# Two passes of a batch loop written out, with the second batch's first norm and queries placed among the first batch's last MLP steps, and a setup loaded in order of use

## The reference

```python
def reference(x, ctx, cond, ...):
    # L0: adaptive norm (scale, bias from silu(cond) @ Wss_q), cross attention to the
    #     context (16 heads of 16; keys, values from an adaptive norm of ctx), residual
    x = _L0(x, ctx, cond)
    # L1: norm, scores of each token against 64 prototypes (q @ k, softmax, @ v),
    #     combined = [norm, evidence, anchor]; router softmax over 3 experts,
    #     h = silu(combined @ e_w1 + b), h @ e_w2, sigmoid gate, output projection, residual
    x = _L1(x, cond, ctx)
    # L2: modulated norm, self attention over 1024 tokens, cross attention, gelu MLP of 1024
    x = _L2(x, cond, ctx)
    # L3: modulated norm, windowed self attention (rolled by 64), cross attention to the
    #     16 best of 64 keys, modulated norm, swiglu MLP: silu(a) * b @ w_m2 + b_m2
    return _L3(x, cond, ctx)
```

## Time and profile before

| what | value |
|---|---|
| median of 3 runs | 1728.73 us (1727.78 to 1730.44) |
| profiled execution | 1729.8 us |
| its span, first to last instruction | 1728.0 us |
| PE busy | 1546.6 us (90%) |
| DVE busy | 1046.0 us (61%) |
| ACT busy | 795.9 us (46%) |
| POOL busy | 356.3 us (21%) |
| instructions in the span | 29083 |

### The profile page before, as it was taken

The page is one execution under the profiler, slowest core; times in us unless marked ns, Lnnn a source line. Parts: engine busy times, 40 slices in busy tenths (PEclk is TensorE's granted clock), DMA queues, the critical chain, the costliest instruction groups (busy, mean ns, idle before and its releaser), DMA issues.

```text
span 1728.0 us, 29083 instructions
## 1 busy us (share of the span) xinstructions
PE 1546.6 (90%) x10441; PEld 909.4 (53%) x10441; DVE 1046.0 (61%) x2935; ACT 795.9 (46%) x1263; POOL 356.3 (21%) x386
## 2 busy tenths in 40 slices
PE   3789998999989998877979999899999889887888
PEld 1536565434444766555754556543444366555566
DVE  1474343899927445799437433479991744569953
ACT  1144331388863542335534434128887354333454
POOL 0050003433006000013205000163300700001230
PEclk9899999899999999999999999899999999999999
DMA  9200005422020000000050000352201000000004
GB/s 322 105 1 1 0 1 135 67 39 39 2 75 1 1 1 2 2 1 1 7 166 1 1 0 1 113 89 39 39 3 58 17 1 1 2 2 1 1 1 146
DMA packets 43340, 64.15 MB, mean 37 GB/s; under 512 B 8634, under 2 KB 32061, under 8 KB 42301
## 3 DMA queue, kind: packets, MB, share of 16 engines
q1 hardware_dynamic: 32845, 40.73, 7.1%
q0 software_dynamic: 8448, 14.96, 5.6%
q10 hardware_dynamic: 1904, 6.55, 1.0%
HBM read 47.28 MB, written 2.10 MB: 29 GB/s over the span
## 4 chain that ended last, share of the span: by engine, by line
PE 41%; issue 38%; DVE 9%; POOL 8%; ACT 3%; DMA 0%; POOLq 0%; ACTq 0%; DVEq 0%
PE ps L936 8%; PE ps L948 7%; PE ps L454 6%; PE ps L921 3%; PE ps L1030 3%; PE ps L1038 3%; PE ps L564 2%; DVE taken L2250 2%; PE ps L1241 2%; PE ps L1096 1%; PE ps L1137 1%; PE ps L572 1%; DVE mxw L2204 1%; POOL rstd L2349 1%; DVE m L2245 1%
## 5 line engine op out<-in xcount | busy, mean ns | idle before, releaser
L2120 DVE TENSOR_REDUCE mm<-ps 128x1 f32<-128x1024 f32 x256 | 310.1, 1223 | 36.7 <-PE ps L921 30.4
L1543 ACT ACTIVATE pt<-ps 128x512 f32<-128x512 f32 x512 | 276.9, 600 | 63.3 <-PE ps L936 54.7
L2349 POOL TENSOR_TENSOR rstd<-ve,minus_half 128x4 f32<-128x4 f32 x32 | 35.4, 1107 | 820.6 <-DVE ve L1854 820.6
L936 PE MATMUL ps<-qx,kx 64*128 64x512 f32 x512 | 192.3, 453 | 1.0 <-ACT pt L1543 1.0
L921 PE MATMUL ps<-kx,qx 48*128 48x512 f32 x512 | 190.4, 452 | 1.7 <-DVE mm L2120 1.5
L948 PE MATMUL ps<-pt,v 128*32 128x256 f32 x2048 | 161.8, 397 | 0.0
L936 PEld LDWEIGHTS ps<-qx,kx 64*128 64x128 f32 x512 | 80.4, 187 | 97.2 <-ACT pt L1543 91.6
L2010 DVE TENSOR_TENSOR rlo<-ring,rhi 128x512 fp32r<-128x512 f32 x48 | 33.2, 692 | 127.5 <-ACT ring L1494 127.5
L921 PEld LDWEIGHTS ps<-kx,qx 48*128 48x128 f32 x512 | 77.0, 188 | 25.3 <-issue 15.4
L948 PEld LDWEIGHTS ps<-pt,v 128*32 128x32 f32 x2048 | 43.4, 109 | 88.1 <-ACT pt L1543 65.3
L1494 ACT ACTIVATE rhi<-ps,mod 128x512 fp32r<-128x512 f32 x48 | 33.1, 690 | 98.9 <-PE ps L727 98.8
(11 more groups left out here) (327 smaller groups left out, 3408.1 us busy)
## 6 DMA issues: line engine op xcount, KB each, us to landing
w<-in_L_xcond_e_w_dram SPq DMA_DIRECT2D x9, 512.0 KB, 7.4
w<-in_L_xcond_e_w_dram SPq DMA_DIRECT2D x3, 1536.0 KB, 11.3
wm<-in_L_xcond_W_mlp_dram SPq DMA_DIRECT2D x4, 1024.0 KB, 8.5
qx<-q_hi POOLq DMA_DIRECT2D x64, 64.0 KB, 2.6
kx<-k_hi POOLq DMA_DIRECT2D x64, 64.0 KB, 2.8
w3a<-in_L_xcond_w_m_dram SPq DMA_DIRECT2D x2, 2048.0 KB, 7.7
s_ada<-in_L_xcond_w_ada_dram ACTq DMA_DIRECT2D x1, 2304.0 KB, 14.4
qx<-q_lo POOLq DMA_DIRECT2D x32, 64.0 KB, 2.7
```

Source lines behind the costliest of these rows:

```text
L936: pe.matmul(ps[:, bank, :], kx[r, p % 4, kc * P:(kc + 1) * P], qx[r, p % 4, half * 512:(half + 1) * 512], start=True, stop=True).then_inc( ...
L1543: act.activation(pt[:, u % 8, half * 512:(half + 1) * 512], ps[:, bank, :], ACT.Exp, scale=QK_SCALE).then_inc(st_read, 1)
L2120: return dve.tensor_reduce(mm[:, p % 2, e, t:t + 1], place(), X, ALU.max).then_inc(ring_read, 1)
L2349: pool.tensor_tensor(rstd[:, k, :], ve[:, k, :], minus_half[:, :], ALU.pow).then_inc(rstd_ready, 1)
```

## The change

- The loops over b are written out in Python on all engines: each wait compares with a constant. `mod`, `v_ctx`, `kT`, `kw` and `rc` are no copies but views of the doubled tiles; `begun` falls away. The router's part of `kw` is loaded into both batches' `kw2`.
- x has 12 tiles instead of 8. Half k of batch b lies in tiles 4 ((2b + k) mod 3) onwards. x of batch 1, first half, is loaded in the setup; its second half when the first half of batch 0's result has left.
- The last steps of batch 0's MLP hold, on PE, `ln(0,0)` of batch 1 at step 14, its first query at 15, its second `ln` at 17, then the output turned, then the second query; on ACT their evictions; on DVE the two statistics at steps 11 and 15 and the two normalises. A last yT goes to a tile of its own, `yT7`.
- The setup loads in another order: ACT's queue brings key and value weights first, then the modulation; SP brings 12 rows, x's first half, the anchor and evidence weights, `load_ra`, x's second half, batch 1's first half. POOL issues the other 17 rows and the 15 constants. PE's and DVE's lists follow that order. `load_ra` is called once more only if a batch follows.
- The evidence products are made once for both batches (the rows of batch 0 in the upper 64, of batch 1 in the lower), and two DMAs on SP copy the half that each batch lacks (`ev_doubled`).

The core of the diff (lines of names and of unchanged products left out):

```diff
-        x = keep("x", [P, T, D])
+        x = keep("x", [P, 3 * TB, D])
...
+        yT7 = at("yT7", [P, KC, BLK], F32, RF + 12 * K1)
...
+        def load_constants(eng):
...
+            for tile, name in ((parity, "c_parity"), (head_mask, "c_head_mask"), (ones_ctx, "c_ones_ctx")):
+                eng.dma_start(tile[:, :], g[name]).then_inc(consts_ld, 16)
...
+            for b in range(B):
+                eng.dma_start(kw2[:, b, :, S:], rows(g["L1_xcond_router_W"][0:D, :])).then_inc(consts_ld, 16)
...
+            load_rows(sp, 0, 12, rows_ld[0])
...
+            load_x(0, 0)
...
+            load_x(0, 1)
+            load_x(1, 0)
+            sp.wait_ge(set_act, 7)
+            sp.dma_start(vw2[S:2 * S, 0, :], vw2[0:S, 0, :]).then_inc(ev_doubled, 16)
+            sp.dma_start(vw2[0:S, 1, :], vw2[S:2 * S, 1, :]).then_inc(ev_doubled, 16)
...
-                sp.wait_ge(w32_done, b * NB * NC_HID + NC_HID)
-                load_ra()
...
+                if b + 1 < B:
+                    sp.wait_ge(w32_done, b * NB * NC_HID + NC_HID)
+                    load_ra()
...
+            pe.wait_ge(s_kv0_ld, 16)
+            pe.wait_ge(set_dve, 9)
...
+            pe.wait_ge(s_ev_ld, 5 * 16)
+            pe.wait_ge(set_dve, 7)
+            for c in range(KC):
+                pe.matmul(ps[:, 7, D:D + E], s_vT[:, c, :, :].rearrange("p b s -> p (b s)"), s_rev[:, c, :], start=c == 0, stop=c == KC - 1)
+            for c in range(KC):
+                ins = pe.matmul(ps[:, 7, 0:D], s_vT[:, c, :, :].rearrange("p b s -> p (b s)"), s_gev[:, c, :], start=c == 0, stop=c == KC - 1)
+            ins.then_inc(set_pe, 1)
+            for e in range(E):
+                for c in range(KC):
+                    ins = pe.matmul(ps[:, 4 + e, :], s_vT[:, c, :, :].rearrange("p b s -> p (b s)"), s_ev[:, e, c, :], start=c == 0, stop=c == KC - 1)
+                ins.then_inc(set_pe, 1)
...
+                    led = i == 0 and b > 0
+                    if not led:
+                        if i == 0:
+                            pe.wait_ge(kpair_ready, 1)
+                        ln(norm, 0)
+                        if i == 0:
+                            pe.wait_ge(wq_ld, 2 * 16)
+                            pe.wait_ge(set_dve, 10)
+                        query(i, 0, col, wq)
+                        if i == 0:
+                            pe.wait_ge(set_act, 7)
+                        ln(norm, 1)
                     pe.wait_ge(qT_ready, b * 2 * N_Q + 2 * i + 1)
                     pe.wait_ge(kpair_ready, b * 2 + i + 1)
+                    if led:
+                        pe.wait_ge(x_final, b * NB)
                     token_scores(0)
-                    linear(6, wq, 0, hT[:, 1], (hT_ready, b * 2 * N_HT + 2 * (col + 1))).then_inc(q_done, 1)
+                    if not led:
+                        linear(6, wq, 0, hT[:, 1], (hT_ready, b * 2 * N_HT + 2 * (col + 1))).then_inc(q_done, 1)
                     token_scores(1)
-                    linear(7, wq, 1, hT[:, 1]).then_inc(q_done, 1)
+                    if not led:
+                        linear(7, wq, 1, hT[:, 1]).then_inc(q_done, 1)
...
                     if n >= NC_HID + 2:
                         down(n - 2)
-                residual(7, 1, True, bank=4)
+                    if b + 1 < B:
+                        if n == 2 * NC_HID - 2:
+                            ln(0, 0, 6, b + 1)
+                        elif n == 2 * NC_HID - 1:
+                            pe.wait_ge(wq_ld, (b + 2) * 2 * 16)
+                            pe.wait_ge(x_final, b * NB + 1)
+                            query(0, 0, 0, wq0, 2, b + 1)
+                        elif n == 2 * NC_HID + 1:
+                            pe.wait_ge(h3_read, n0 + 2 * NC_HID)
+                            ln(0, 1, 4, b + 1)
+                if b + 1 < B:
+                    pe.wait_ge(qT_ready, (b + 1) * 2 * N_Q + 1)
+                    residual(7, 1, True, bank=2)
+                    query(0, 1, 0, wq0, 6, b + 1)
+                else:
+                    residual(7, 1, True, bank=4)
...
+            for tile, name in ((s_kvc, "L2_xcond_W_kvc"), (s_kv3, "L3_xcond_w_kv"), (s_k1, "L1_xcond_Wk"), (s_v1, "L1_xcond_Wv")):
+                act.dma_start(tile[:, :, :], rows(g[name])).then_inc(s_kv_ld, 16)
+            act.dma_start(s_q1[:, :, :], rows(g["L1_xcond_Wq"])).then_inc(s_q_ld, 16)
...
+            act.dma_start(s_kv0[:, :, :], rows(g["L0_xcond_Wkv"])).then_inc(s_kv0_ld, 16)
...
+                    if n == 2 * NC_HID - 2 and b + 1 < B:
+                        ln(0, 0, (mod2[:, b + 1, :], M_SC_Q, M_SH_Q), 6, b + 1)
                 product_hi(2 * NC_HID - 1)
+                if b + 1 < B:
+                    query(0, 0, C_BQ0, 2, b + 1)
                 mlp3_out(1)
+                if b + 1 < B:
+                    ln(0, 1, (mod2[:, b + 1, :], M_SC_Q, M_SH_Q), 4, b + 1)
...
+            dve.wait_ge(consts_ld, 15 * 16)
...
+            dve.wait_ge(x_ld[0][0], 16)
+            statistics(0, 0, 0)
+            normalise(0, 0, 0)
...
+            dve.wait_ge(x_ld[0][1], 48)
+            statistics(0, 0, 1)
+            dve.wait_ge(set_pe, 9)
+            for m in range(KC):
+                ins = dve.tensor_scalar(kT2[:, 0, m, :, :], ps[:, 1, m * P:(m + 1) * P].rearrange("p (b s) -> p b s", b=B),
+                                        colT[:, C_BK0 + m:C_BK0 + m + 1], None, ALU.add)
+            link(ins)
+            pair_keys(0, 0)
+            normalise(0, 0, 1)
+            dve.wait_ge(set_pe, 10)
+            context_values(0, 3)
+            dve.wait_ge(set_pe, 11)
+            plus_biases(M_HB, 2, 0, E, RH // P)
+            plus_biases(M_HB + MC, 2, E, 1, KC)
...
+            dve.wait_ge(set_dve, 10)
...
-                dve.tensor_copy(mod[:, :], mod2[:, b, :])
-                dve.tensor_copy(v_ctx[:, :, :, :], v_ctx2[:, b, :, :, :])
-                dve.tensor_copy(kT[:, :, :, :], kT2[:, :, :, b, :])
-                dve.tensor_copy(kw[:, :, 0:S], kw2[:, :, b, :])
-                dve.tensor_copy(rc[:, :], rc2[:, b, :]).then_inc(begun, 1)
...
+                    if b + 1 < B:
+                        if n == NC_HID + 3:
+                            dve.wait_ge(x_ld[b + 1][0], 16)
+                            statistics(b + 1, 0, 0)
+                        elif n == NC_HID + 4:
+                            normalise(b + 1, 0, 0)
+                        elif n == 2 * NC_HID - 1:
+                            dve.wait_ge(x_ld[b + 1][1], 48)
+                            statistics(b + 1, 0, 1)
                 product_lo(2 * NC_HID - 1)
-                residual(7, 1, 4).then_inc(x_final, 1)
-                dve.wait_ge(x_final, b * NB + NB)
+                if b + 1 < B:
+                    normalise(b + 1, 0, 1)
+                residual(7, 1, 2 if b + 1 < B else 4).then_inc(x_final, 1)
...
+            load_rows(pool, 12, 18, rows_ld[1])
...
+            load_rows(pool, 18, len(vectors), rows_ld[1])
+            load_constants(pool)
...
+                if b == 0:
+                    pool.wait_ge(ev_doubled, 32)
+                else:
+                    pool.wait_ge(w32_done, b * NB * NC_HID)
```

518 lines of the change are left out of this document (248 added, 270 removed).

## The result

The changed kernel takes 1698.81 us (median of 4 runs, 1693.57 to 1702.0) against 1729.22 for the kernel before (median of 4 beside them, 1727.78 to 1730.44): ratio 0.9829, 95% interval 0.981 to 0.9848. So by the two ratios the change gives 30 and 26 us where 33 were forecast. The profiled execution took 1699.16, its span is 1697.3.

What follows compares the result with a forecast made beforehand. Setup was taken as bound by a chain of DMA, late PE work and a norm, the boundary by PE idling; 22.2 + 10.7 = 32.9 us off 1729.8 gave 1696.9, forecast as 1695.5 measured, range 1684 to 1706.

Steps and rivals of the forecast that it cites:

- Setup, 22.2 forecast: Setup: first query of the first batch moves from 81.6 to 59.4 us, a gain of 22.2 us.
- 52.1: Setup: second half of x lands at 52.1 us, 57.2 less 5.1 for SP's filled gap; bounds 47 and 57.
- I take that as the wait that ends last: Setup: landing of x's second half ends last; DVE work behind it takes 6.4 us, before the first query.
- PE's own list: Setup: modulation lands at 25 to 29, 22 us of work end at 47 to 51, leaving 5 to 10 us spare.
- 3.3 of DVE for the modulation and s_ctxT: Setup: DVE's modulation and s_ctxT take 3.3 us within the 22 us from PE's modulation rows through the evidence products.
- POOL's DMAs: Setup: 32 row and constant loads at 546 ns each, 17.5 us, issued by 21, landed by 30 us.
- Rivals (3): Setup: POOL's DMAs are slow with many small rows; 1713 us at 1.5 us each, 1703 at 1.2; chance 0.08.
- (5): Setup: kernel slower than before if each POOL DMA exceeds 2.0 us; about 1764 us at 3.1 each; chance 0.02.
- Boundary, 10.7 forecast: Between batches: first token scores come at 904.9 instead of 915.6, a gain of 10.7 us; bounds 8 and 13.
- Taking the second query out of them gives nothing back: Boundary score steps: DVE's maxima set the pace either way, so removing the second query loses 0 us.
- The rest. 0, at most 3.: Elsewhere: written-out loops and constant waits give 0 us in attention and MLP steps, at most 3 us gained.
- Rival (4): Boundary gives half, 5 us: PE's added work stays and the yT wait remains; 1701 us; chance 0.10.

Runs made afterwards that it cites:

- the last kernel of the study: Changed kernel with early x, reordered norms, query between scores, early pairs, POOL's copy held, and modulation rows turned before the anchor-weights wait: 1682.52 us, 0.973.
- the pairs early: Changed kernel with the second query back between the token scores and DVE forming key pairs ahead of the residual add: 1694.45 us, 0.9802.
- POOL held back: Changed kernel with early x, first norm behind context norm, query between scores, early pairs, and POOL's values copy waiting for the pairs: 1682.72 us, 0.9734.

## Why the prediction was right, and where it wasn't

The time (1695.5 forecast, 1698.8 and 1701.8 measured, both in the range) and its sign were right, and both places of gain are where it put them. Some steps were not.

- **Setup, 22.2 forecast, 20.7 measured at the first query.** x landed at 54.0 instead of 52.1; the list behind it took 6.0 us for 6.4, ACT and the start 1.0 for 0.9. (The terms of the list as the forecast gives them add up to 6.3.) The end of the sum holds; that it does so this closely is partly luck. Its reason for 52.1 is off: 57.2 less 5.1 for the filled gap. From 30 to 40 us the engines did move 1.84 MB more (370 GB/s for 186), but from 5 to 30 they moved 0.75 MB less (365 for 395), which the sum left out; the difference is 2.9 us at 380 GB/s. And with the constants back on SP, x comes at 55.4, so that gap was worth 1.5 us of x and about none of the time. As the traces have it, 17.9 of the 20.7 us stand at the end of the evidence products (start 12.6 earlier, and 5.3 for half as many) and 2.8 between there and the first query. No run undoes these one by one. The early place of the norms is no part of the gain: with the norms behind the biases, as before, the kernel is faster still.
- **"I take that as the wait that ends last"** was right for the changed kernel, and the runs show what kind of wait it is: not x as data but x as a place in DVE's list (7.5 us at the token scores from reordering alone).
- **PE's own list "47 to 51", "5 to 10 us to spare".** The last modulation weights landed at 27.4, in the forecast's 25 to 29, but that isn't what set the start of the rows at 27.97. PE had waited until 17.00 for the last bias row, which POOL issues now, and then ran 11 us of products without a gap; these rows are a term that the forecast didn't price, and it cost nothing here (the last kernel of the study still waits there until 17.10, and no run moved that). Rows at 27.97 plus its 22 us make 50, but the evidence products end at 55.2 and ACT's copies at 56.4 for 52.5. The step that failed is "3.3 of DVE for the modulation and s_ctxT": its size is right (39.11 to 42.31), but DVE had the first block's statistics and normalise ahead of it and started 3.2 us late; PE waited 4.74 us and then ran keys and values partly at the low clock (0.70 granted from 42 to 50), 7.4 us for about 6. To spare were 3.6 us (56.4 to 60.0).
- **POOL's DMAs**: 0.52 to 0.60 us each but for the first and the last two (0.74 and 0.73), as the earlier trace rows had it; done by 19.6, and the last constant landed near 31 for 30. Rivals (3) and (5) fell. As to the Trainium skill's stall of GpSimd DMAs beside DVE copies ("SBUF — State Buffer", section "SBUF: two separate sides"): no issue of these 32 shows it, but DVE ran few copies in that time, so this says little about the rule.
- **Boundary, 10.7 forecast.** The token scores came 11.4 us earlier, near the step's own sum. "Taking the second query out of them gives nothing back" failed: 3.3 us went again, because the query had kept PE at its full clock through the waits for DVE; of the signs of the forecast, "no PE idle above 1 us but the one for yT" and "clock at full" failed with it (2.48 us twice, 0.63). Net 8.0, the lower of the bounds, though for another reason than the one given there. And not all of it belongs to the move: of the 8.0 (182.5 to 174.5) the loop written out has 1.5 by itself, 3.9 by the second key scores (45.6 to 41.7), and without the moved work the kernel has 4.2.
- **"The rest. 0, at most 3."** In the traces the first batch shows nothing for the loop written out. The 5.6 us of its span are the boundary (1.5), the two top-k stretches (4.2 and 2.8) and what follows the last mark (1.2), less 4.1 that the other stretches took more.
- **Rival (4)**, half of the boundary, fits the size better than its reason: PE's added work did stay (3.3 us more up to the end of the last down product), but that was in the forecast's sum, with 3.65.

## What to carry to other kernels

Ask of each released engine whether it waits for data or for a place in another engine's list: a late transfer costs only what stands behind it in the list, and moving that cost nothing here. Work that stands where TensorE would wait for another engine may be what keeps its clock up; when you take it out, price the gap at the low clock, not at nothing. When two stretches of the same instructions differ by more than the effect sought, measure the effect between marks in the trace and not by the median.

## What the hardware showed that I had not expected

- **DVE held by POOL.** The two DVE operations that form the key pairs take 0.51 us in the kernel before and 2.41 beside POOL's subtraction in the changed kernel. One of the two takes 2.21 us and the other 0.28:

```profile
L1893 DVE TENSOR_TENSOR kpair<-kT,parity x2: 278/1244/2211, 877.4 to 879.5; 128x128 f32<-128x128 f32 x2
```

The second starts at 879.5, when POOL's instruction (876.09, 3.37 us) ends: by the trace DVE stood until the end rather than running slower beside it. With the pairs early, the first of the two starts ahead of POOL's cast and takes 0.29; the second takes 1.78, until just behind the cast's end (878.06). DVE's residual add (876.19), one of whose inputs is in PSUM, takes 1.28 us beside the same subtraction, and 1.29 with the boundary undone, where POOL is idle then. With POOL held back both key pairs take 0.49 us together. By the Trainium skill ("SBUF — State Buffer", section "SBUF: two separate sides") the two engines lock a shared pair of ports for a whole instruction, and a DVE operation with two SBUF inputs is one that needs it against a GpSimd operation that reads SBUF; both hold here, and the trace agrees.
- **A shorter wait pays twice.** The first query took 5.12 and 6.24 us in the two profiles of the changed kernel, where PE had been idle for 1.9 and 2.7 us and then 2.8 ahead of it, and 3.67 in the six kernels where evidence products and norm ran until 1.3 us ahead of it. In the four other kernels in which it waits for the second half of x it took 6.07 to 6.73.
- **DMA landing under load.** With three queues busy from 5 us on, a 3 KB constant took 12.1 us to land, for 8.3 before, and the 2304 KB of `s_ada` 22.0 for 14.4. The two also changed place: the constant is issued by POOL now, and `s_ada` stands behind 1.75 MB more of its own queue, so how much of it is load is not shown.
